# Later wait for the split dense weights, and batch 1's score pairs before the unit's last output projection, in an attention and gated-dense kernel on one core

## What is computed

```python
x = x + attn(layernorm(x), w_qkv, w_o)
x = x + ffn(layernorm(x), weight, bias, centroids, assignments)

# attn: 32 query heads, 8 key/value heads, head size 128, causal, with a bias of -slope[head] * sqrt(i - j)
qkv = h @ w_qkv                                   # 512 x (4096 + 1024 + 1024)
p = softmax(q @ k.T / sqrt(128) + bias)           # a query head shares the keys of its group of 4
out = (p @ v) @ w_o                               # 4096 x 512

# ffn: a dense layer whose rows and columns are switched off where no cluster is hit
hits = softmax(h @ centroids.T / 0.1) > 0.01      # 64 clusters
out = where(any(hits, 1)[:, None] & any(hits, 0)[assignments][None, :], h @ weight.T + bias, 0)
```

## Time and profile before

| | us |
|---|---|
| median of 3 runs (lowest, highest) | 1237.29 (1236.43, 1238.93) |
| the profiled execution | 1236.09 |
| its span, first to last instruction | 1234.4 |
| TensorE busy (share of the span) | 1223.9 (99%) |
| ScalarE busy | 745.1 (60%) |
| VectorE busy | 708.6 (57%) |
| GpSimd busy | 588.5 (48%) |
| mean granted TensorE clock | 0.998 of full speed |

### The profile page before, as it was taken

How to read it: one execution, slowest core, us unless ns; L and a number is a source line. 1 busy time by engine, 2 the same in 40 slices (tenths; PEclk the granted TensorE clock), 3 DMA queues, 4 the chain that set the end, 5 groups by cost and what they waited for, 6 DMA issues and landing times.

```text
span 1234.4 us, 20645 instructions
## 1 busy us (share of the span) xinstructions
PE 1223.9 (99%) x5860; PEld 1027.4 (83%) x5860; DVE 708.6 (57%) x1633; ACT 745.1 (60%) x2164; POOL 588.5 (48%) x522
## 2 busy tenths in 40 slices
PE   8999999999999999999999999999999999999998
PEld 7888888888888888888888888888888888878887
DVE  7766554545555555555554545555555555567677
ACT  4866556666655565665556666655565665566553
POOL 4533646336452656326463465436463374644323
PEclk9999999999999999999999999999999999999999
DMA  6553545445453444444543454444454454622303
GB/s 205 175 167 112 171 136 170 145 136 178 137 170 132 141 160 163 151 144 138 168 154 127 154 169 153 154 135 159 136 173 144 136 169 141 201 94 98 98 28 136
DMA packets 210010, 180.71 MB, mean 146 GB/s; under 512 B 12608, under 2 KB 162880, under 8 KB 209984
## 3 DMA queue, kind: packets, MB, share of 16 engines
q1 hardware_dynamic: 205952, 167.55, 41.4%
q0 software_dynamic: 4032, 12.85, 3.4%
HBM read 101.45 MB, written 78.91 MB: 146 GB/s over the span
## 4 chain that ended last, share of the span: by engine, by line
PE 95%; DVE 2%; issue 1%; ACT 1%; POOL 1%; DMA 0%; SPq 0%; DVEq 0%; POOLq 0%
PE ps L1598 92%; PE ps L1623 1%; PE ps L1633 0%; DMA acc<-in_L_attn_hidden_states 0%; PE ps L1728 0%; DVE prob L1137 0%; DVE stats L1088 0%; POOL wo_lo L610 0%; PE ps L1739 0%; DVE acc L1208 0%; DVE xnT L1144 0%; ACT prob L896 0%; PE ps L1747 0%; PE ps L1609 0%; ACT prob L883 0%
## 5 line engine op out<-in xcount | busy, mean ns | idle before, releaser
L1598 PE MATMUL ps<-xnT,wqkv_hi 128*128 (+2 forms) x1560 | 481.2, 390 | 1.9 <-issue 1.9
L674 POOL TENSOR_TENSOR ring<-ring_whole,pT_hi 128x512 fp32r<-128x512 f32 x189 | 245.0, 1296 | 366.2 <-ACT pT_hi L874 362.7
L1598 PEld LDWEIGHTS ps<-xnT,wqkv_hi 128*128 128x128 f32 x1560 | 290.5, 188 | 60.8 <-issue 2.3
L1598 PE MATMUL ps<-xnT,wqkv_lo 128*128 (+1 forms) x780 | 303.3, 389 | 0.0
L883 ACT ACTIVATE prob<-prob,negmax 128x256 f32<-128x256 f32 (+1 forms) x384 | 176.7, 461 | 151.8 <-DVE negmax L1231 120.3
L1598 PE MATMUL ps<-wo_hi,oT_hi 128*128 128x512 f32 x512 | 200.4, 391 | 0.0
L1598 PE MATMUL ps<-wo_lo,oT_hi 128*128 128x512 f32 x512 | 199.6, 390 | 0.0
L1598 PE MATMUL ps<-wo_hi,oT_lo 128*128 128x512 f32 x512 | 199.3, 389 | 0.0
L874 ACT ACTIVATE pT_hi<-ring_whole 128x512 fp32r<-128x512 f32 x189 | 117.8, 624 | 127.2 <-DMA ring_whole<-turned 90.8
L1208 DVE TENSOR_TENSOR acc<-ps,acc 128x512 f32 (+1 forms) x128 | 88.3, 690 | 155.2 <-PE ps L1598 155.2
L896 ACT ACTIVATE prob<-prob,rinv 128x256 f32<-128x256 f32 (+1 forms) x384 | 150.1, 462 | 39.1 <-DVE rinv L1237 39.1
(11 more groups left out here) (155 smaller groups left out, 1737.5 us busy)
## 6 DMA issues: line engine op xcount, KB each, us to landing
turned<-ring_whole SPq DMA_DIRECT2D x189, 256.0 KB, 2.1
ring_whole<-turned SPq DMA_DIRECT2D x189, 256.0 KB, 2.9
turned_v<-vT SPq DMA_DIRECT2D x32, 256.0 KB, 2.0
turned_s<-prob SPq DMA_DIRECT2D x32, 256.0 KB, 2.0
prob<-turned_s SPq DMA_DIRECT2D x32, 256.0 KB, 2.7
turned_s<-vT SPq DMA_DIRECT2D x32, 256.0 KB, 2.0
vT<-turned_s SPq DMA_DIRECT2D x32, 256.0 KB, 3.9
vT<-turned_v SPq DMA_DIRECT2D x31, 256.0 KB, 2.7
```

The lines of the kernel that those rows point to most:

```text
L674: pool.tensor_tensor(ring_slot(c), whole_slot(c), pT_hi[:, c % 2, :].bitcast(F32), ALU.subtract).then_inc(pT_lo_done, 1)
L1598: ins = pe.matmul(dst, l, r, start=start and m == 0, stop=stop and m == n - 1)
```

## The change

- TensorE: in units with no `p` or with `p == 1`, `scores(u, 1, 0)` and `scores(u, 1, 1)` go ahead of `project_out(u, 3)`.
- TensorE: the wait for `wT_done` moves from the second projection step of units 30 and 31 to just ahead of `cluster_logits`. SP: the load of `w_raw` is issued right behind unit 28's last turned tile, ahead of `turn_v(29)`; the other dense loads stay.
- `w_qkv` is laid out anew on the host before the launch, so that a group's part of 128 rows is one block, and each load of it is one DMA. The semaphore counts follow.
- TensorE: `project_first` makes three outputs (k and the first two query heads) with all passes of the hi weights ahead of the passes of the lo weights; before it was two (k and one head).
- ScalarE: in `second_unit`, `pT_hi_part` 1 and 2 each go one step ahead of `normalise(u - 1, 2)` and `exps(u - 1, 5)`; at the start `first_w_hi(2)` goes ahead of the first two `ln_hi`.
- Tail: chunk 0 of `dense(2, 1)` goes ahead of `logits_by_token(3)` on TensorE, and `dense_part(2, 2, 0)` ahead of `finish(0, 4)` and its wait on VectorE.

```diff
@@ -407,11 +407,7 @@
         @block.sync
         def _(sp):
             def load_qkv(g, c):
-                rows = w_qkv[c * P:(c + 1) * P, :]
-                slot, done = first_raw(c), first_loaded[c]
-                sp.dma_start(slot[:, 0:HPG * D], rows[:, bass.ds(g * (HPG * D), HPG * D)]).then_inc(done, 16)
-                sp.dma_start(slot[:, HPG * D:HPG * D + D], rows[:, bass.ds(g * D + NH * D, D)]).then_inc(done, 16)
-                sp.dma_start(slot[:, HPG * D + D:QKV_W], rows[:, bass.ds(g * D + (NH + NKV) * D, D)]).then_inc(done, 16)
+                sp.dma_start(first_raw(c), w_qkv[bass.ds(g * HID + c * P, P), :]).then_inc(first_loaded[c], 16)
 
             def load_o(g, h):
                 rows = w_o[bass.ds(g * (HPG * D) + h * D, D), :]
@@ -482,10 +478,7 @@
             def last_qkv(g, c):
 
                 sp.wait_ge(raw_split, g * (2 * NC) + c - 1)
-                rows = w_qkv[c * P:(c + 1) * P, :]
-                kv = rows[:, NH * D:].rearrange("p (a n) -> p a n", a=2)[:, :, bass.ds(g * D, D)]
-                sp.dma_start(raw[:, c % 2, 0:HPG * D], rows[:, bass.ds(g * (HPG * D), HPG * D)]).then_inc(last_loaded[c % 2], 16)
-                sp.dma_start(raw[:, c % 2, HPG * D:QKV_W].rearrange("p (a n) -> p a n", a=2), kv).then_inc(last_loaded[c % 2], 16)
+                sp.dma_start(raw[:, c % 2, :], w_qkv[bass.ds(g * HID + c * P, P), :]).then_inc(last_loaded[c % 2], 16)
 
             def unit(v):
                 turn_v(v)
@@ -543,11 +536,11 @@
                     unit(g * QUADS + q)
                 last_of_group(g)
             unit(UNITS - QUADS)
+            sp.wait_ge(qkv_mm, PROJ_OUTS * (UNITS - QUADS + 1))
+            sp.dma_start(w_raw[:], w_ffn.rearrange("(t p) d -> p t d", p=P)).then_inc(wc_loaded, 16)
             turn_v(UNITS - 3)
             scores_out(UNITS - 3, 0)
             scores_in(UNITS - 3, 0)
-            sp.wait_ge(qkv_mm, PROJ_OUTS * (UNITS - QUADS + 1))
-            sp.dma_start(w_raw[:], w_ffn.rearrange("(t p) d -> p t d", p=P)).then_inc(wc_loaded, 16)
             sp.dma_start(c_raw[:, 0:NC, :], cents.rearrange("(t p) n -> p t n", p=P)).then_inc(wc_loaded, 16)
             sp.dma_start(assigned[:].bitcast(I32),
                          assign.rearrange("(a n) -> a n", a=1).broadcast_to([CLUSTERS, HID])).then_inc(assign_loaded, 16)
@@ -628,10 +621,7 @@
                 pool.tensor_tensor(lo, source, hi.bitcast(F32), ALU.subtract).then_inc(wT_done, 1)
 
             def load_qkv(g, c):
-                rows = w_qkv[c * P:(c + 1) * P, :]
-                kv = rows[:, NH * D:].rearrange("p (a n) -> p a n", a=2)[:, :, bass.ds(g * D, D)]
-                pool.dma_start(raw[:, c % 2, 0:HPG * D], rows[:, bass.ds(g * (HPG * D), HPG * D)]).then_inc(raw_loaded[c % 2], 16)
-                pool.dma_start(raw[:, c % 2, HPG * D:QKV_W].rearrange("p (a n) -> p a n", a=2), kv).then_inc(raw_loaded[c % 2], 16)
+                pool.dma_start(raw[:, c % 2, :], w_qkv[bass.ds(g * HID + c * P, P), :]).then_inc(raw_loaded[c % 2], 16)
 
             def load_o(g, h):
                 pool.dma_start(raw[:, h % 2, 0:HID], w_o[bass.ds(g * (HPG * D) + h * D, D), :]).then_inc(raw_loaded[h % 2], 16)
@@ -651,9 +641,9 @@
                         sum_scores(g * QUADS - 1, 0)
 
                     if c < 2:
-                        pool.wait_ge(raw_loaded[c % 2], g * 64 - 32)
+                        pool.wait_ge(raw_loaded[c % 2], g * 48 - 32)
                     else:
-                        pool.wait_ge(last_loaded[c % 2], g * 32)
+                        pool.wait_ge(last_loaded[c % 2], g * 16)
                     split(raw[:, c % 2, :], wqkv_hi[:, c, :], wqkv_lo[:, c, :], g * (2 * NC) + SETUP + c + 1)
 
             def split_o(g, h, part=None):
@@ -662,7 +652,7 @@
                 elif isinstance(g, int) and g == 0:
                     pool.wait_ge(first_o_loaded[h % 2], 16 * (h // 2 + 1))
                 else:
-                    pool.wait_ge(raw_loaded[h % 2], g * 64 - 32 + 16 * (h // 2 + 1))
+                    pool.wait_ge(raw_loaded[h % 2], g * 48 - 32 + 16 * (h // 2 + 1))
                 if part != 1:
                     split_hi(raw[:, h % 2, 0:HID], wo_hi[:, h, :])
                 if part != 0:
@@ -994,10 +984,10 @@
                 pT_hi_part(u, 0)
                 exps(u - 1, 3)
                 exps(u - 1, 4)
+                pT_hi_part(u, 1)
                 normalise(u - 1, 2)
-                pT_hi_part(u, 1)
+                pT_hi_part(u, 2)
                 exps(u - 1, 5)
-                pT_hi_part(u, 2)
                 proj_hi(u, 3)
                 oT_hi_part(u, 0)
                 normalise(u - 1, 3)
@@ -1018,7 +1008,7 @@
                 normalise(u, 1)
 
             def first_w_hi(c):
-                act.wait_ge(first_loaded[c], 48)
+                act.wait_ge(first_loaded[c], 16)
                 act.activation(wqkv_hi[:, c, :], first_raw(c), ACT.Copy).then_inc(w_hi_done, 1)
 
             act.wait_ge(dist_sq, 1)
@@ -1026,9 +1016,9 @@
             ln_root(0)
             first_w_hi(0)
             first_w_hi(1)
+            first_w_hi(2)
             ln_hi(0, 0, 0)
             ln_hi(0, 1, 0)
-            first_w_hi(2)
             ln_hi(0, 2, 0)
             ln_hi(0, 3, 0)
             first_w_hi(3)
@@ -1561,9 +1551,9 @@
             last_cluster_hits()
             dve.wait_ge(sel_mm, 1)
             dve.tensor_scalar(cluster_sel[:], ps[0:CLUSTERS, PV[0], 0:P], 0.0, None, ALU.is_gt).then_inc(csel_ready, 1)
+            dense_part(2, 2, 0)
             dve.wait_ge(sel_mm, 2)
             finish(0, 4)
-            dense_part(2, 2, 0)
             dense_part(2, 2, 1)
             finish(4, 4)
             dense_part(2, 2, 2)
@@ -1627,12 +1617,12 @@
 
                 pe.wait_ge(ln_hi_done, TPQ)
                 x_hi, x_lo = [lambda c, part=part: xnT[:, 0, part, c, :] for part in range(2)]
-                cols = (HPG * D, 0)
+                cols = (HPG * D, 0, D)
 
                 def one(i, c, w, x, start=False, stop=False):
                     return pe.matmul(ps[:, proj_bank(0, i), :], w[:, c, cols[i]:cols[i] + D], x(c), start=start, stop=stop)
 
-                for i in range(2):
+                for i in range(3):
                     for c in range(NC):
                         if i == 0:
                             pe.wait_ge(w_hi_done, c + 1)
@@ -1780,7 +1770,7 @@
                                 pe.wait_ge(added, u * QTILES + i - 1)
                         elif i > 2:
                             pe.wait_ge(qk_lo_done, 4 if is_first(u) and i == PROJ_OUTS - 1 else u * 5 + i - 2)
-                        if not is_first(u) or i > 1:
+                        if not is_first(u) or i > 2:
                             project(u, i)
                         elif i == 0:
                             project_first()
@@ -1788,7 +1778,6 @@
                         if i == 1:
                             pe.wait_ge(v_lo_done, u)
                         if i == 1 and p is not None:
-                            pe.wait_ge(wT_done, NC + 1)
                             pe.wait_ge(cl_exp_done, p + 1)
                             pe.wait_ge(dense_out, p * TPQ + TPQ)
                         if lag <= i < CHUNKS - 2 + lag:
@@ -1821,6 +1810,7 @@
                     scores(u, 0, 0)
                     scores(u, 0, 1)
                 if p is not None:
+                    pe.wait_ge(wT_done, NC + 1)
                     cluster_logits(p, u)
                 if attn:
                     project_out(u, 1)
@@ -1842,14 +1832,14 @@
                     dense(p, 2)
                     scores(u, 1, 0)
                     scores(u, 1, 1)
+                if p != 0:
+                    scores(u, 1, 0)
+                    scores(u, 1, 1)
                 if attn:
                     pe.wait_ge(added, u * QTILES + 2)
                     project_out(u, 3)
                 if p == 0:
                     dense(p, 3)
-                else:
-                    scores(u, 1, 0)
-                    scores(u, 1, 1)
 
             def second_unit(u):
 
@@ -1954,8 +1944,9 @@
             pe.wait_ge(added, u * QTILES + QTILES)
             for j in range(TPQ):
                 ln_transpose(7, j)
+            dense(2, 1, (0,))
             logits_by_token(3)
-            dense(2, 1)
+            dense(2, 1, (1, 2, 3))
             dense(2, 2, (0, 1))
             pe.wait_ge(hits_done, QUADS - 1)
             any_hits = ps[0:CLUSTERS, PV[0], 0:P]
@@ -1995,6 +1986,12 @@
         a = np.ascontiguousarray(inputs[name])
         if name == 'L0_attn_hidden_states':
             a = a.reshape(TOK, HID)
+        elif name == 'L0_attn_w_qkv':
+            kv = NH * D
+            a = np.ascontiguousarray(np.stack([np.concatenate([a[:, g * HPG * D:(g + 1) * HPG * D],
+                                                               a[:, kv + g * D:kv + (g + 1) * D],
+                                                               a[:, kv + (NKV + g) * D:kv + (NKV + g + 1) * D]], axis=1)
```

(1 more changed line is left out.)

## The result

The changed kernel took **1260.63 us** (median of 4 runs, 1259.09 to 1262.07); the kernel before took 1236.86 (4 runs, 1235.0 to 1238.93) in the same comparison. The ratio is 1.0203, 95% interval 1.0188 to 1.0218: slower by 23.8 us. 1261 was forecast, within 1246 to 1270. The profiled execution took 1260.19 us, its span is 1258.3.

A forecast was written before the change was run, and what follows sets the result against it. TensorE, busy 1223.9 of 1234.4 us, was taken as the bound. Terms 13.1 + 9.4 + 4.6 - 3.1 - 0.3 + 0.6 = +24.3 us on 1236.1 gave 1260.4, stated as 1261 us, range 1246 to 1270.

The forecast's parts named there:

- bank of `scores(u,1,1)`: Moved score pairs on TensorE wait for VectorE's transpose to free the bank: 0.45 us in each of 29 units, +13.1 us.
- (a): Second unit of seven groups: GpSimd's split of output weights comes 1.35 us later, project_out(u,0) waits; 1.35 us each, +9.4 us.
- (b): First unit of seven groups: chunk 5's reload and `ring` 5 come later against TensorE; 0.65 us each, +4.6 us.
- wait for wT_done: Near unit 30, TensorE's wait and the clock's fall go (-3.5 us), layernorm tiles come 0.4 us late: -3.1 us.
- front: Start of the kernel: two `ring` waits go and more projections fill TensorE, partly offset by other waits: -0.3 us.
- tail: End of the kernel: a dense quarter fills a 0.3 us gap, unit 31's late add_bias costs 0.9: +0.6 us.
- The queue behind `add_out`: VectorE's add_out(u,3) stays ahead of add_bias, so exps, `ring` and turned tiles come 1.35 us later against TensorE.
- Only the direct wait is paid: Rival, chance 0.16: in the loop only the wait at the bank costs, later engines absorb the shift; 1246 us.
- The bank free in time: Rival, chance 0.05: the transpose ends within 0.90 us of the last by-key matmul's start, nothing lost there; 1232 us.
- The loop isn't touched: Rival, chance 0.03: `p != 0` leaves units with no `p` out of the pairs' move; about 1234 us.
- The clock swings: Rival, chance 0.04: each of 29 waits is followed by a 1.2 GHz stretch of 1.4 us, another 40 us; 1301 us.

The follow-up runs named there:

- e5: The changed kernel with turn_scores(u,1) ahead of add_out(u,2) on VectorE: 1258.68 us, ratio to the kernel before 1.0192.
- e3: The changed kernel with add_bias(u,3) and add_bias(u,4) ahead of add_out(u,3) on VectorE: 1244.84 us, ratio to the kernel before 1.0073.
- e2: The kernel before with only the score pairs of batch 1 moved ahead of project_out(u,3): 1261.48 us, ratio 1.0203.
- e7: e6 with the load of w_raw also ahead of turn_v(29) on SyncE: 1233.06 us, ratio to the kernel before 0.9982.
- e8: The kernel before with the front's edits alone (ScalarE's order in second_unit, first_w_hi(2) earlier, three outputs projected first): 1234.40 us, ratio 0.9996.
- e9: The kernel before with only the query, key and value weights laid out in one piece, one DMA per chunk: 1236.76 us, ratio 1.0005.
- e1: The changed kernel with the score pairs of batch 1 back behind project_out(u,3): 1231.54 us, ratio to the kernel before 0.9966.
- e4: e3 with the first head of project_out(u,3), three matmuls, between the two score pairs: 1232.07 us, ratio to the kernel before 0.997.
- e6: The kernel before with only the wait for wT_done moved to just ahead of cluster_logits: 1233.72 us, ratio 0.999.
- e10: The kernel before with the tail's two edits alone (a quarter of dense(2,1) and dense_part(2,2,0) earlier): 1234.32 us, ratio 0.9987.

## Why the prediction was right, point by point

The measured terms are differences of TensorE's starts, unit by unit, between the two traces. Together they give 23.9 us; the last matmul starts 23.93 us later (1254.07 against 1230.14).

| step | forecast | measured |
|---|---|---|
| bank of `scores(u,1,1)`, 29 times | +13.1 | +13.4 |
| (a) second units | +9.4 | +8.5 |
| (b) first units | +4.6 | +4.6 |
| wait for wT_done, unit 30 | -3.1 | -2.6 |
| front | -0.3 | -0.7 |
| tail | +0.6 | +0.6 |
| not in the sum (small gaps in other units) | 0 | +0.1 |

- **The sum.** That it comes within 0.4 us (24.3 against 23.9) owes something to luck: (a) was forecast 0.9 too high and the front 0.4, the bank 0.3 and the wait 0.5 too low, and that nearly cancels. And 1260.4 with the 1.2 us of the median on top is 1261.6, not the 1261 that was said; against a range of 24 us neither matters.
- **Bank: right in size, wrong in one reason.** Units 3 to 29 cost 0.45 us each (12.15), unit 2 0.36, unit 31 0.85. Unit 31 was taken as one of the 29; there the transpose came later still, and e5 took 0.5 us of that away. The sentence "VectorE is then still on add_out" reads as the cause of the late transpose, and e5 refutes that for the loop; the number was safe because it came from the measured starts of both engines. "There is no gap" in the other 26 units was not quite so: units 9, 17 and 25 of the kernel before are 35.70 to 35.79 us long, which is the lag behind `wo_lo` that (a) names itself.
- **The queue behind `add_out`: right**, and the largest finding: e3 gives 15.8 us for (a), (b) and what else hangs on the shift. (a) was 0.9 too large: the shift is 1.26 us (2.29 - 1.03), not 1.35, since the score instructions follow `add_out` after 0.61 us, not 0.65, and take 1.37, not 1.41; 7 times 0.09 is 0.6 of it. All seven ended 0.10 us behind the end of `wo_lo`. That (b) comes out to 0.1 us is partly luck: the seven first units lost between 0.36 and 0.98 us each, and in e2 it is others of the seven that lost most.
- **wT_done: the mechanism right, what comes back mis-sized.** At the wait itself 3.8 us went (39.37 - 35.56), more than the 3.5 charged; 1.4 us or so of it is the fall of the clock in the one trace of before. But "the layernorm tiles of unit 30, which I put 0.4 us behind TensorE" cost 0.63, `ring` 2 with the slow pair behind it 0.4, and one more slow pair 0.1: 1.2 in all (the interval from unit 30 to 31 is 52.27 where e7 has 51.04).
- **Front and tail: right within their bounds, the tail in part by luck.** e8 and e9 can't be told from nothing. The tail's +0.6 was a gain of 0.3 and a loss of 0.9. Without the moved pairs the edited tail (e1) is 0.6 us shorter than that of before (100.58 against 101.15), and after's is 1.2 us longer than e1's, unit 31's bank left out; in e3, without the shift, that 1.2 us is gone (100.58 again). So both terms were 0.3 too small, and that cancelled.
- **"Only the direct wait is paid"** would have been e3's time (1244.84, its 1246). It takes one moved call on VectorE to make it true. **The bank free in time** decided at 0.90 us and the transpose ended at 1.24; with 0.68 us more work between the pairs, and e3's order on VectorE, e4 comes out at that rival's 1232. **The loop isn't touched** is out: all 27 loop units are longer.
- **The clock swings: not so.** 28 waits for the bank, 12 for `ring` and 7 for `wo_lo`, of 0.2 to 0.75 us each, left the granted clock of the whole profiled span at 1.000, the level of 2.4 GHz. (Two of the other three runs of after are recorded at 0.998; one fall as long as that near 1082 in before makes about that, 47 of them would leave 0.94.) The rule of the Trainium skill ("TensorE: Matmul & The Clock Gate", section "A second HAM failure mode: psum-queue depth-cycling") is not borne out by waits of this size and spacing.

## What to carry to other kernels

A consumer moved ahead of other work loses that work as its cover: before moving it, take the producer's end minus the consumer's new start from two engines' start times, and leave just that much other work in between (e4: three matmuls). Then look at the engines that drain the moved work in order: here half of the loss, 15.8 us, was one accumulation that kept its place ahead of the score instructions, and moving that one call takes it away without touching TensorE. And a stall that sits behind a delayed engine is worth less once something else delays TensorE as well (e2), so gains of single edits don't add up across a change that slows the loop.

## What was not expected of the hardware

**VectorE's start behind a matmul.** In units 3 to 29, the loop, `turn_scores` starts 0.52 us behind the start of the 512-column matmul that it waits for, whether VectorE has been idle for 2.70 us or comes straight from another instruction (e5 and after, above). With 0.72 us for the transpose and 0.05 to TensorE, the bank comes back 1.29 us after that start. But it is 0.43 us in units that are written out, wherever nothing else holds the transpose: for batch 0 of units 1, 2 and 31 in all twelve traces, and for batch 1 in unit 31 of e5, where TensorE and VectorE show:

```profile
1187.89 0.39 PE L1588 MATMUL ps<-qT_hi,kT 128*128 128x512 f32 x1
```

```profile
1188.32 0.72 DVE L1164 STREAM_TRANSPOSE vT<-ps 128x512 f32<-128x512 f32 x1 [0.24 <-PE ps L1588]
```

That is where e5's 0.42 us came from: the price was read in unit 1 and used in the loop. It is also why unit 2 lost 0.36 us and not 0.45. What costs the 0.09 us in the loop, no run shows.

**The clock falls without a long wait.** In the profiles of e2, e7 and e9 it falls to half in the tail, at the start of the dense matmuls that follow the cluster logits (in e9 at the last of the logits). TensorE of e7 by window (the granted clock is the third number from the end), and its timeline, whose last row is cut off where the window asked for ends:

```profile
1202.00:1205.50 3.50, 3.50 (x33) 3.50 (x33) 1.88 (x6) 3.01 (x10) 0.00 (x0) 0.98 0.00 0
1205.30:1208.80 3.50, 3.50 (x10) 2.82 (x10) 2.87 (x11) 2.06 (x10) 0.00 (x0) 0.51 0.00 0
```

```profile
1205.11 0.31 PE L1739 MATMUL ps<-cT,wqkv_hi 128*128 128x128 f32 x1
1205.26 0.27 PE L1740 MATMUL ps<-cT,wqkv_lo 128*128 128x64 f32 x1
1205.35 1.63 PE L1598 MATMUL ps<-xnT 128*128 128x512 f32 x3
```

TensorE is busy all the while, with 3.6 us of narrow matmuls of 128 and 64 columns (logits, from 1201.74), and then runs 7 dense ones at 1.2 GHz, 0.43 us apart. Its tail is 102.59 us long where e6 and e8 have 101.0: 1.6 us. Three of the six profiles without the tail's edits show it (e2, e7, e9) and three don't (before, e6, e8); of the six with a quarter of `dense(2,1)` ahead of the logits (after, e1, e3, e4, e5, e10) none does. That would fit e10's gain being larger than the gap it fills, but a profile is one execution. The mean clock on record for every run says a little more. Of the 23 runs of the kernel before beside e9 and e10, the five at 0.997 or less took 1237.5 to 1239.7 us, the other 18, at 0.999 or 1.000, 1233.3 to 1236.7: much of the spread is the clock. e1 and e4, with the tail's edits and without the wait, have none below 0.999 in 12 runs; e10, with the edits and the wait, has three at 0.998 in 12. No run was made that tells the two places apart.

**The same wait, with and without the drop.** In e8, where the wait for `wT_done` was left in, TensorE's timeline and window show:

```profile
1079.92 0.39 PE L1598 MATMUL ps<-xnT,wqkv_lo 128*128 128x512 f32 x1
1082.02 0.70 PE L1598 MATMUL ps<-xnT,wqkv_hi 128*128 128x512 f32 x2 [1.72 <-issue]
```

```profile
1082.50:1086.00 3.50, 3.50 (x17) 2.84 (x16) 1.64 (x8) 1.93 (x8) 3.18 (x3) 1.00 0.00 0
```

1.87 us lost in starts and the clock stays at 1.00, where 2.1 us in before brought 0.51; it stays at 1.00 behind the same wait in e9 (1.76 us), e10 (1.36) and e2 (1.14) too. So the 1.4 us that the sum took for the clock there was the price in one execution, not in each.
